# P·V of a self-attention head in three bursts instead of two, in a one-core cross-attention block kernel

## The reference

```python
def _attention(xq, xkv, wq, wk, wv, wo, bo):
    q = (xq @ wq).reshape(B, S, N_HEADS, D_HEAD)
    k = (xkv @ wk).reshape(B, T, N_HEADS, D_HEAD)
    v = (xkv @ wv).reshape(B, T, N_HEADS, D_HEAD)
    attn = jnp.einsum('bihd,bjhd->bhij', q, k) * D_HEAD ** (-0.5)
    attn = jax.nn.softmax(attn, axis=-1)
    out = jnp.einsum('bhij,bjhd->bihd', attn, v).reshape(B, S, D_ATTN)
    return out @ wo + bo

h = _layernorm(x, ln1_g, ln1_b)
x = _attention(h, h, sa_wq, sa_wk, sa_wv, sa_wo, sa_bo) + x
h = _layernorm(x, ln2_g, ln2_b)
x = _attention(h, cond_emb, ca_wq, ca_wk, ca_wv, ca_wo, ca_bo) + x
h = _layernorm(x, ln3_g, ln3_b)
p = h @ ff_w1 + ff_b1
a, gate = (p[..., :D_FF], p[..., D_FF:])
return a * jax.nn.gelu(gate, approximate=False) @ ff_w2 + ff_b2 + x
```

## Time and profile before

| | |
|---|---|
| median of three runs | 1064.27 us |
| the profiled execution: its time | 1063.16 us |
| its span, first to last instruction | 1061.4 us |
| mean granted TensorE clock | 0.998 of full speed |
| TensorE busy | 1025.7 us, 97% |
| VectorE busy | 828.3 us, 78% |
| ScalarE busy | 626.0 us, 59% |
| GpSimd busy | 300.7 us, 28% |
| P·V matmuls (L622) | 8192 records, 240.2 us |
| P·V on the chain that ended last | 21% |

### The profile page before, as it was taken

One profiled execution on the slowest core, in us unless ns is written; L12 is line 12 of the kernel. 1 busy time (PEld: TensorE's weight loads), 2 busy tenths in 40 slices (PEclk: granted clock), 3 DMA queues, 4 the chain that ended last, 5 costly groups with the idle time before them and its releaser, 6 DMA issues.

```text
span 1061.4 us, 28582 instructions
## 1 busy us (share of the span) xinstructions
PE 1025.7 (97%) x12258; PEld 834.4 (79%) x12258; DVE 828.3 (78%) x971; ACT 626.0 (59%) x1127; POOL 300.7 (28%) x268
## 2 busy tenths in 40 slices
PE   7989999999998999999999999998999999999998
PEld 5777777777776778777777777876688888888887
DVE  4768888889889878888888889999768898555433
ACT  4746665666676656666666666676655645443322
POOL 5103322322332123423223222322313336711000
PEclk9999999999999999999999999999999999999999
DMA  8897677667666956575785657598210001100001
GB/s 188 235 199 166 136 152 156 125 134 139 144 134 122 204 121 141 116 161 119 147 183 115 140 119 153 116 213 182 47 62 21 1 11 40 51 1 20 20 2 40
DMA packets 179646, 121.38 MB, mean 114 GB/s; under 512 B 142656, under 2 KB 159552, under 8 KB 175040
## 3 DMA queue, kind: packets, MB, share of 16 engines
q1 hardware_dynamic: 179520, 119.55, 51.6%
HBM read 56.60 MB, written 12.58 MB: 65 GB/s over the span
## 4 chain that ended last, share of the span: by engine, by line
PE 81%; DVE 8%; ACT 5%; issue 3%; POOL 1%; DMA 1%; SPq 0%; DVEq 0%; POOLq 0%; ACTq 0%
PE W L622 21%; PE SC L597 18%; PE W L634 10%; PE SC L686 8%; PE W L570 7%; PE W L696 4%; PE W L580 4%; PE W L862 3%; ACT OTF L950 3%; PE SC L674 2%; DVE nmax L1164 2%; DVE PR L1169 2%; PE W L849 1%; ACT PR L942 1%; POOL PR L512 1%
## 5 line engine op out<-in xcount | busy, mean ns | idle before, releaser
L942 ACT ACTIVATE PR<-SC,nmax 128x1024 f32<-128x1024 f32 x256 | 285.8, 1116 | 224.4 <-DVE nmax L1164 223.9
L1164 DVE TENSOR_REDUCE nmax<-SC 128x1 f32<-128x1024 f32 x256 | 308.2, 1204 | 108.3 <-PE SC L597 108.1
L1169 DVE STREAM_TRANSPOSE PR<-PR 128x1024 f32<-128x1024 f32 x256 | 315.2, 1231 | 0.1
L464 POOL TENSOR_TENSOR X<-f_raw,X 128x512 f32<-128x512 f32 x128 | 164.9, 1289 | 498.3 <-ACT f_raw L961 498.2
L597 PE MATMUL SC<-QKS 128*128 128x512 f32 x1024 | 297.1, 416 | 4.9 <-ACT PR L942 4.8
L622 PE MATMUL W<-PR,V 32*64 32x256 f32 x8192 | 240.2, 379 | 4.4 <-DMA V<-scratch_v 2.4
L597 PEld LDWEIGHTS SC<-QKS 128*128 128x128 f32 x1024 | 184.2, 188 | 64.9 <-issue 23.0
L622 PEld LDWEIGHTS W<-PR,V 32*64 32x64 f32 x8192 | 187.0, 132 | 51.3 <-issue 23.9
L634 PE MATMUL W<-wo,OTF 128*128 128x256 f32 x512 | 134.4, 385 | 7.9 <-ACT OTF L950 7.0
L634 PEld LDWEIGHTS W<-wo,OTF 128*128 128x128 f32 x512 | 93.9, 189 | 36.9 <-ACT OTF L950 20.7
L961 ACT ACTIVATE f_raw<-W,rden 128x256 f32<-128x256 f32 x256 | 106.5, 473 | 0.1
(11 more groups left out here) (128 smaller groups left out, 1401.5 us busy)
## 6 DMA issues: line engine op xcount, KB each, us to landing
QKS<-QKT SPq DMA_DIRECT2D x64, 512.0 KB, 6.3
V<-scratch_v SPq DMA_DIRECT2D x128, 256.0 KB, 5.0
QKS<-QKT SPq DMA_DIRECT2D x128, 128.0 KB, 4.8
scratch_v<-VST SPq DMA_DIRECT2D x32, 256.0 KB, 4.7
wo<-in_L_xattn_sa_wo_dram SPq DMA_DIRECT2D x64, 64.0 KB, 3.0
f_raw<-in_L_xattn_ff_w_dram SPq DMA_DIRECT2D x12, 256.0 KB, 3.1
X<-in_x_dram SPq DMA_DIRECT2D x4, 512.0 KB, 5.0
w_raw<-in_L_xattn_sa_wk_dram SPq DMA_DIRECT2D x16, 128.0 KB, 2.9
```

The costliest lines, as they stand in the source:

```text
L464: nc.gpsimd.tensor_tensor(xs, f_raw[:, k % 2, :], xs, ALU.add).then_inc(p_x, 1)
L942: nc.scalar.activation(PR[:, NT * s + t, :], SC[t % 2][:, :], ACT.Exp, bias=nmax[:, t % 4:t % 4 + 1], accum_out=den[:, s, t:t + 1]).then_i ...
L1164: V.tensor_reduce(nmax[:, t % 4:t % 4 + 1], SC[t % 2][:, :], AX, ALU.max, negate=True).then_inc(d_max, 1)
L1169: V.transpose(tile, tile).then_inc(d_tr, 1)
```

## The change

The bursts are at tiles 2, 3 and 4 instead of 2 and 4. They have 12, 10 and 10 key blocks instead of 16 and 16. The matmuls, their order among themselves and their number stay the same. `LAST_BURST` is 4 as before, so ScalarE's order is the same.

```diff
-        BURSTS = {2: (0, 16), 4: (16, 32)}
+        BURSTS = {2: (0, 12), 3: (12, 22), 4: (22, 32)}
         LAST_BURST = max(BURSTS)
```

## The result

The changed kernel takes 1081.64 us (median of four runs, 1079.72 to 1083.29) against 1064.61 us before (median of four; the three runs shown ahead of the prediction gave 1064.27). The ratio is 1.0161, with a 95% interval of 1.0141 to 1.0181. The forecast was 1074.5 us in a range up to 1081. The sign was right, the size was too small by 7 us.

A forecast was written before the change was run, and what follows sets the result against it. TensorE, busy for 97% of the span, was taken to bound the kernel. 28 x 0.36 + 2 x 0.22 = 10.5 us on 1063.16 made 1073.7, by the median 1074.8; it said 1074.5 us, range 1070.5 to 1079 (8 in 10: 1069 to 1081).

The forecast's parts named there:

- What bounds: TensorE, busy 97% of the span: its path from tile 2's scores to the gather gets 0.36 us longer a head.
- The bursts: Behind tiles 2, 3 and 4: 2.78, 2.34 and 2.34 us on the chain, plus 0.26 for the last one's signal.
- the line: Cost of a burst on TensorE: 0.18 us plus 27.0 ns for each record, from lengths 48, 80, 128 and 256.
- The scores behind a burst: Four score matmuls right behind a burst take 1.11 us instead of 0.93; tile 4's now pay the added 0.18 too.
- a passage: TensorE's switch from whole array to 32 x 64 pieces and back; one added in heads 1 to 31, 0.36 us.
- A: Rival: the whole standstill of the weight loads at bursts counts, 0.74 us a head, 1086 us; chance 0.08.
- B: Rival: only half of the added switch of tiling is lost, 0.18 us a head, 1069.7 or 1067.5 us; chance 0.10.
- rival C: Faster: short bursts end before the instruction queue empties, gaining 0.61 us a head and paying 0.36, 1056.8 us; chance 0.04.
- The two conditions of the gather: Gather into OTF needs the last burst's signal, at 9.94 us after the change, and ScalarE's readout, ready at 9.82.
- Heads 12, 9 and 26: Heads paying less because VectorE holds them: 0 in head 12, 0.22 us each in heads 9 and 26.
- The stops: TensorE's unexplained halts inside bursts, 1.40 us in head 29 and 0.60 in head 1: expected as often as before.
- the sum: Added time over all heads: 28 x 0.36 + 2 x 0.22 = 10.5 us.

The follow-up runs named there:

- the cut: From the second pair of heads on, QKS<-QKT transfers move 64 columns instead of 512 or 1024: 1062.2 us on the kernel before, 1074.9 us on the changed kernel.

## Why the prediction was wrong

**What bounds.** Right. TensorE's path through the bursts carries the time, the gather is released by the last burst in plain heads, and nothing gave the added time back.

**The bursts.** Right to the hundredth: 2.78, 2.34, 2.34 us, from four lengths in the trace of before. The two runs with bursts of 64 and 160 are on the line too (1.91 and 4.50). It fails at 8 records (0.59).

**The scores behind a burst.** Mis-sized. I took 1.11 us, from 2.04 - 0.93, and it is 1.14, twice, so 11.10 instead of 11.03 for the head. The 0.93 was too much for the second four of a row of eight: 2.04 - 1.14 = 0.90. So a passage is 0.43 us, not 0.36, and that is 28 x 0.07 = 2 us. The rivals A, B and C are out: the idle weight loads of 0.74 us count to somewhat more than half, tile 4's scores paid like tile 3's, and the bursts of 80 ran on the line of the longer ones.

**The two conditions of the gather.** Right for the change, with 0.12 us to spare: in head 16 the readout ends at 434.03, the last burst's signal comes at 434.14. The experiments with 8, 16, 8 and with 20, 12 blocks show that it was as near as that.

**Heads 12, 9 and 26.** Right: 13.29 us after 13.28 in head 12, and in heads 9 and 26 0.29 where I said 0.22.

**The stops.** This is the step that failed: "I expect such stops with the new order as often as before." They went from 2.0 to 6.7 us, so 4.7 us that the sum had at nothing. I had seen 1.40 and 0.60 us in the trace and named a thin supply of instructions under rival C, but only as a thing that short bursts might relieve, not as one that a new order could make worse. That the stops hang on QKS<-QKT is shown by the cut, and that they sit at packet ends by the counts. Why the packet that is late after the change was in time before, the packets' starts show for two heads. In head 15 the packet comes equally late in both kernels, 7.0 to 7.1 us after the head's first QKS<-QKT transfer is issued. TensorE gets to matmul 5035 2.5 us after its start before the change, just in time, and 1.6 us after it now: then it stands until 2.3 us are over. In head 19 the packet started ahead of the transfers before the change and behind them after it. So where the packet ends fall among bursts and transfers decides, and that I hadn't worked out. Why the packet of head 19 starts ahead of the transfers in the one order only stays open.

In the spans the change cost 16.2 us where the sum had 10.5. The stops make 4.7 of the difference and the scores 1.9; heads 9 and 26 add 0.1, and head 1 takes 0.9 off (I had it at +0.36, it came to -0.5). The measured median is 7.1 us over the forecast: 5.7 of it is this difference, the rest lies in how the medians sit against the profiled executions.

## What to carry to other kernels

Bursts of different lengths in one trace, and the work behind them, give nearly the whole price of changing the array's tiling without an experiment: 0.36 us from the trace before, 0.43 measured. Multiplied by the heads, it is what parting a burst costs where TensorE's path holds the gather. Before a burst is moved or resized, look at the scores behind it as well: a burst of 4 blocks more before tile 3 cost 0.70 us a head with no passage added. A stop for which the profile names nothing, in a stream of very short instructions, can be a sign that instruction packets come just in time. Count the matmuls up to it, and look when the packets start. A new order beside large transfers made more such stops here (2.0 to 6.7 us).

## What the runs showed of the hardware

- The stretch between the last weight load of one tiling and the first of the other was, but for some with stops or other waits, 0.35 to 0.37 us into the pieces and 0.38 to 0.39 us back, in every kernel. The Trainium skill, TensorEngine Tiling (Array Packing), section Tiling Modes, has it that a change of mode drains TensorE. The trace agrees that there is a standstill. What it costs on the chain was 0.43 us for the pair.
- TensorE's stops inside the bursts fell at packet ends, multiples of 127 matmuls with their weight loads apart, and cost a head 0.2 to 4.6 us (the longest single gap was 3.0). They followed QKS<-QKT (512 and 128 KB transfers in flight during the bursts of odd heads) and stayed when the V loads were cut. They ended 2.2 to 3.2 us after the start of a packet of TensorE's instruction queue.
